# A two-pass graph layer on one core: loads issued ahead of ScalarE's sums, VectorE's share of the row sums from 5 to 4 groups of 16, and long and short stripes in turn in the second pass

## The chip, the cores and the metric

The kernel runs on one core of a Trainium2 chip. The metric is the device time of one execution in microseconds (us), lower is better. A change of under about 0.2% can't be told from no change here.

## The reference

Only this much of it matters (N = 8192 rows, 128 features, all float32):

```python
def _L0_gnn_ref(x, adj, W):
    A_hat = adj + jnp.eye(adj.shape[0], dtype=adj.dtype)
    d_inv_sqrt = jnp.sum(A_hat, axis=1) ** (-0.5)
    A_norm = d_inv_sqrt[:, None] * A_hat * d_inv_sqrt[None, :]
    support = x @ W.T
    out = A_norm @ support
    return jax.nn.relu(out)
h = jnp.maximum(_layernorm(x, axis=-1), 0.0)
x = x + _L0_gnn_ref(h, adj, L0_gnn_W)
return x
```

The matrix adj is 8192 x 8192 float32, 268 MB, and can't be kept on the chip. A row of the output needs the row sums of all columns' rows (the factor on the right), so a block of adj can enter the product only when the sums of the rows with its columns' numbers are known.

## The kernel before, in words

**Cells and stripes.** The rows are cut into 16 stripes u of 512 rows. A stripe and a column group v (512 columns) meet in a cell (u, v) of 1.05 MB: 128 partitions with 16 groups (C = 16) of 128 values each. A whole stripe is 16.8 MB. A cell is transposed by VectorE in two halves (L663, `adjT<-...`), and TensorE then does four 128x512 products with it (L460), each of which the trace records as two MATMUL rows, since the data is float32.

**First pass.** For each stripe in turn all its 16 cells are read, since its row sums need them all. The cells are of three kinds. `far` cells (right of the band, v > u+2) are only summed, and dropped. `left` cells (v < u) are summed and also multiplied, since the sums of their column's rows are known. `near` and `thirds` hold the three cells of the band (v = u, u+1, u+2), which are kept on the chip and multiplied later, each column of them when its scale is known.

**Second pass.** The far cells of stripes 0 to 12 (91 of the 256) are read again (`again` pieces), in the order of stripes that AGAIN_ROWS gives, and multiplied. A stripe that is complete is turned back, scaled, rectified, added to x and stored, while the next ones run (`finish`, `rows_back`, `combine`, `relu`, and a last addition on GpSimd).

**Pieces and slots.** far, left and again cells arrive in numbered pieces m of at most 3 cells' worth in three buffers, slot0 to slot2, in turn (in the second pass `thirds` is a fourth). Half of every piece (quarters 0 and 1 of the partitions) is loaded from SyncE's DMA queue, the other half (quarters 2 and 3) from ScalarE's. `load_piece(queue, quarters, m)` first waits, then issues. SyncE does nothing but these loads and the stores. ScalarE issues its halves between its sums: `next_piece(m)` issues its half of piece m + 2, and after the last piece of a stripe the halves of near and thirds (L292, L298), which wait for VectorE's transposes of older band cells.

**Who sums what.** A far piece is summed by ScalarE alone (L504). In left pieces and in near VectorE sums the first DVE_C of the 16 groups (L648), ScalarE the others, one instruction a group (L515, a 3-cell group is 128x384). A left slot is free when ScalarE has summed it (`act_freed`) and VectorE has transposed and summed it (`dve_freed`).

**End of a stripe.** ScalarE sums near, raises `act_sums` (L564), and VectorE folds the sums (`fold_parts`, L683 to L693), TensorE adds them over partitions (L431), VectorE, GpSimd (L389) and VectorE make the scale and scale support. Only then may the column's band cells be multiplied. In stripes 1 to 8 these band cells stand ahead of the stripe's left cells in the product order, in stripes 9 to 15 up to four left cells stand ahead of them.

**ScalarE's queue.** Instructions of an engine run in the order of the code, its DMA issues included. An issue that has to wait holds up the sums behind it.

Of the kernel before, what the change touches and what calls it, by code (L numbers as in the profile page):

```python
# [28 lines left out]
def gnn_kernel(nc: bass.Bass, x: bass.AP, adj: bass.AP, w: bass.AP, out: bass.AP):  # L29
# [13 lines left out]
    AHEAD = 2  # L43
    HALVES = 2
    TURNS = 3
    BANKS = 5
    DVE_C = 5
    FIRST = 4
    JUNKS = 3
    XC = 4  # L50
# [1 line left out]
    EPS = 1e-5  # L52
    CHAIN_X = 6
    FAR_ROWS = NB - 1 - BAND
    AGAIN_ROWS = [0] + list(reversed(range(1, FAR_ROWS)))

    adj_v = adj.rearrange("(bb u r) (b j) -> u b r bb j", bb=B, u=NB, b=B)
    adj_far = adj.rearrange("(bb u r) (b j) -> u r bb b j", bb=B, u=NB, b=B)
# [33 lines left out]
    AGAIN = len(landing)  # L92
    for u in AGAIN_ROWS:
        again[u] = []
# [12 lines left out]
    by_act = [sum(landing[k][0] != "again" for k in range(m + 1)) for m in range(len(landing))]  # L107
# [18 lines left out]
    stripe_at[NB] = len(order)  # L126
    rest = [(u, v, m) for u in AGAIN_ROWS for m in again[u] for v in range(landing[m][2], landing[m][2] + landing[m][3])]
    order += rest[:FIRST]
# [3 lines left out]
    def group(u, v):  # L132

        return u if v <= u + BAND else NB + AGAIN_ROWS.index(u)

# [6 lines left out]
    masked_by = [sum(2 if far[k] or k == FAR_ROWS else 1 for k in range(u + 1)) for u in range(NB)]  # L142
    finals = [u for u in range(FAR_ROWS, NB)] + AGAIN_ROWS

# [8 lines left out]
    with ctx:  # L153
# [6 lines left out]
        def sem(name):  # L160
            return ctx.enter_context(nc.semaphore(name))
# [53 lines left out]
        act_freed, dve_freed = sem("act_freed"), sem("dve_freed")  # L215
# [13 lines left out]
        def piece(m):  # L229

            n = landing[m][3]
            return slot[slot_of[m]][:, :C * n * CELL].rearrange("p (c j) -> p c j", c=C)

        def far_block(m):
            kind, u, bb, n, v, cells = landing[m]
            return slot[slot_of[m]][:, :n * B * cells * CELL].rearrange("p (a k) -> p a k", a=n)
# [26 lines left out]
        def transposed(n):  # L263

            return HALVES * (n + 1)

        def load_piece(queue, quarters, m):

            before = before_in_slot[m]
            if AHEAD <= m < AGAIN + AHEAD:  # L270
                queue.wait_ge(act_freed, by_act[m - AHEAD])
            if before is None:
                if slot_of[m] == SLOTS:
                    queue.wait_ge(t_done, transposed(column_at[NB - 1] + BAND))
            elif landing[before][0] == "again":
                kind, u, v, n = landing[before][:4]
                queue.wait_ge(t_done, transposed(place[u, v + n - 1]))
            else:
                queue.wait_ge(act_freed, by_act[before])
                if landing[before][0] == "left":  # L280
                    queue.wait_ge(dve_freed, by_dve[before])
            if landing[m][0] == "far":
                load_far(queue, quarters, m)
            else:
                load_cells(queue, quarters, m)
# [196 lines left out]
        @block.scalar  # L482
        def _(act):
            def layernorm(b):
                act.wait_ge(stats_ok, b // (TX // R) + 1)
                if b >= 2:
                    act.wait_ge(hT_ps, b - 1)
                for r in range(R):
                    t = b * R + r
                    nc.scalar.activation(h[b % 2][:, r, :], support[:, t, :], ACT.Relu, bias=shift[:, t:t + 1],  # L490
                                         scale=rstd[:, t:t + 1]).then_inc(h_ok, 1)

            def next_piece(m):

                load_piece(act, (2, 3), m + AHEAD)
                if m + AHEAD in last_piece:
                    load_kept(act, (2, 3), last_piece[m + AHEAD])

            def far_sums(m):
                u = landing[m][1]  # L500
                act.wait_ge(ld_slot[slot_of[m]], landed[m])
                for a in range(landing[m][3]):
                    at = landing[m][2] + a + (B if landing[m][4] > u + BAND + 1 else 0)
                    ins = nc.scalar.activation(far_block(m)[:, a, :], far_block(m)[:, a, :], ACT.Copy,  # L504
                                               accum_out=far_sum[u % 2][:, at:at + 1])
                ins.then_inc(act_freed, 1)
                next_piece(m)

            def late_sums(cells, u, k, before):
                n = cells.shape[2]  # L510
                for c in range(DVE_C, C):
                    at = before * (C - DVE_C) + c - DVE_C
                    if at >= JUNKS:
                        act.wait_ge(junk_done, at - JUNKS + 1)
                    nc.scalar.activation(junk[at % JUNKS][:, :n], cells[:, c, :], ACT.Copy,  # L515
                                         accum_out=part[u % 2][:, k, c:c + 1]).then_inc(junk_done, 1)

            def left_sums(m, k, before):
                act.wait_ge(ld_slot[slot_of[m]], landed[m])
                late_sums(piece(m), landing[m][1], k, before)  # L520
                act.wait_ge(junk_done, (before + 1) * (C - DVE_C))
                act.sem_inc(act_freed, 1)
                next_piece(m)

            def keep(u):
                act.wait_ge(used, transposed(last_of[u]))
                nc.scalar.activation(acc[:, u, :], bank[u % BANKS][:], ACT.Copy).then_inc(kept_acc, 1)

            def relu(n):
                act.wait_ge(y_sum, n + 1)  # L530
                for r in range(R):
                    t = finals[n] * R + r
                    ins = nc.scalar.activation(y[n % 2][:, r, :], y[n % 2][:, r, :], ACT.Relu, scale=dinv[:, t:t + 1])  # L533
                ins.then_inc(y_ok, 1)

            for q in range(XC):
                for b in (2, 3):
                    act.dma_start(support[b * Q:(b + 1) * Q, q * TX:(q + 1) * TX, :],
                                  x_v[b, :, q * TX:(q + 1) * TX, :]).then_inc(ld_x[q], 16)
            for m in range(AHEAD):  # L540
                load_piece(act, (2, 3), m)
            act.wait_ge(ident_ok, 9)
            summed = 0
            for s in range(NB):
                if s >= 2:
                    act.wait_ge(total_ok, s - 1)
                if s == 0:
                    for b in range(NB):
                        layernorm(b)
                        if b % 4 == 3:  # L550
                            far_sums(far[0][b // 4])
                    for m in far[0][NB // 4:]:
                        far_sums(m)
                else:
                    for m in far[s]:
                        far_sums(m)
                for k, m in enumerate(left[s]):
                    left_sums(m, k, summed)
                    summed += 1
                act.wait_ge(ld_near[s % 2], 16 * B * (s // 2 + 1))  # L560
                late_sums(near[s % 2][:, :, :min(2, NB - s) * CELL], s, len(left[s]), summed)
                summed += 1
                act.wait_ge(junk_done, summed * (C - DVE_C))
                act.sem_inc(act_sums, 1)  # L564
                if s >= BAND + 1:
                    keep(s - BAND - 1)
            rectified = stored = 0
            for m in range(AGAIN + AHEAD, len(landing)):
                while rectified < done_by(m):
                    relu(rectified)  # L570
                    rectified += 1
                while stored < done_by(m - 1):
                    store(act, (2, 3), stored)
                    stored += 1
                load_piece(act, (2, 3), m)
                if slot_of[m] == SLOTS and before_in_slot[m] is None:
                    load_xin(act, (2, 3), 0)
                    load_xin(act, (2, 3), 1)
            while stored < NB:
                if rectified < NB:  # L580
                    relu(rectified)
                    rectified += 1
                store(act, (2, 3), stored)
                stored += 1
# [3 lines left out]
        def _(dve):  # L588
# [61 lines left out]
            def transposes(n):  # L650
# [14 lines left out]
                if m is not None and v == landing[m][2] + landing[m][3] - 1:  # L665
                    if landing[m][0] == "left":
                        early_sums(piece(m), u, left[u].index(m), DVE_C).then_inc(dve_freed, 1)

            def kept_sums(u):
                n = min(2, NB - u)  # L670
                dve.wait_ge(ld_near[u % 2], 16 * B * (u // 2 + 1))
                ins = early_sums(near[u % 2][:, :, :n * CELL], u, len(left[u]), DVE_C)
                if u + BAND < NB:
# [148 lines left out]
```

## Time and profile before

| | |
|---|---|
| time, median of 3 runs | 1297.64 us (1297.23 to 1299.93) |
| profiled execution's own time | 1299.58 us |
| its span, first to last instruction | 1297.8 us |
| TensorE busy | 987.8 us (76%) |
| VectorE busy | 842.5 us (65%) |
| ScalarE busy | 531.8 us (41%) |
| moved by DMA | 377.11 MB, mean 291 GB/s |
| granted TensorE clock, mean | 0.894 |

The profile gives busy times, waits and what ended them, the chain of work that ended last, and DMA rates, for the whole span or for a stretch of it. The median is 1.9 us under the profiled execution's time. The first far piece of stripes 1 to 9 lands at about 92, 140, 189, 237, 288, 340, 397, 451 and 507 us, and the second pass runs from about 975 us to the end.

### The profile page before, as it was taken

The numbers are of one execution on the slowest core, as the hardware profiler recorded it, in microseconds if no ns is written. First come the engines' busy times: TensorE is split into PE (matmuls) and PEld (weight loads), VectorE is DVE, ScalarE is ACT, GpSimd is POOL, SyncE is SP. The second block draws the span as 40 slices with busy tenths as digits, with TensorE's granted clock in tenths as the row PEclk, the third lists the DMA queues.
The fourth block names the chain that finished last, engine by engine and source line by source line (L and its number), as shares of the span: only waits on it lengthen the run. The fifth ranks groups of instructions, "written<-read, shape, count | busy, mean of one in ns | idle before, by whom it ended". The sixth has DMA issues, their size and how long they took to land.

```text
span 1297.8 us, 8958 instructions
## 1 busy us (share of the span) xinstructions
PE 987.8 (76%) x2363; PEld 450.4 (35%) x2363; DVE 842.5 (65%) x958; ACT 531.8 (41%) x1596; POOL 52.6 (4%) x61
## 2 busy tenths in 40 slices
PE   1632334755767675678898999899999989999997
PEld 0531112322323232333343444344444434444443
DVE  5441342554646655676788888788877767777775
ACT  2875654753746537182646453654401100000000
POOL 3000000000000000000000000000000110000000
PEclk9866766877888988789898999999999999999999
DMA  9589999999999998999999999998969999999991
GB/s 307 224 291 335 365 325 338 340 323 292 323 323 295 338 267 265 274 274 287 268 312 272 297 252 250 291 304 256 272 165 312 302 326 320 324 340 299 331 318 27
DMA packets 289858, 377.11 MB, mean 291 GB/s; under 512 B 11152, under 2 KB 269328, under 8 KB 289808
## 3 DMA queue, kind: packets, MB, share of 16 engines
q1 hardware_dynamic: 144976, 188.31, 49.7%
q10 hardware_dynamic: 144832, 188.24, 48.1%
q8 instruction: 19, 0.31, 0.1%
q14 instruction: 31, 0.25, 0.1%
HBM read 372.31 MB, written 4.19 MB: 290 GB/s over the span
## 4 chain that ended last, share of the span: by engine, by line
PE 35%; DMA 29%; ACT 14%; ACTq 8%; issue 7%; DVE 5%; SPq 2%; POOLq 0%; POOL 0%; DVEq 0%
PE bank L460 34%; DMA slot<-in_adj_dram 27%; ACT junk L515 8%; ACTq L298 5%; ACT slot L504 5%; DVE adjT L663 4%; DMA thirds<-in_adj_dram 2%; ACTq L251 1%; ACTq L259 1%; ACT acc L490 1%; ACTq L292 1%; SPq L332 1%; DVE part L648 1%; SPq L251 1%; PE pre L443 0%
## 5 line engine op out<-in xcount | busy, mean ns | idle before, releaser
L460 PE MATMUL bank<-adjT,support 128*128 128x512 f32 x2048 | 942.5, 621 | 215.2 <-DVE adjT L663 215.2
L460 PEld LDWEIGHTS bank<-adjT,support 128*128 128x128 f32 x2048 | 403.3, 200 | 731.5 <-issue 725.2
L663 DVE STREAM_TRANSPOSE adjT<-slot 128x1024 f32<-128x1024 f32 x380 | 458.9, 1230 | 294.4 <-DMA slot<-in_adj_dram 204.9
L515 ACT ACTIVATE junk<-slot 128x384 bf16<-128x384 f32 (+2 forms) x495 | 233.4, 473 | 285.6 <-issue 128.0
L504 ACT ACTIVATE slot<-slot 128x6144 f32<-128x6144 f32 (+11 forms) x56 | 166.3, 2970 | 91.3 <-DMA slot<-in_adj_dram 54.1
L533 ACT ACTIVATE near<-near,dinv 128x128 f32<-128x128 f32 x64 | 20.2, 390 | 337.4 <-DVE adjT L663 140.2
L663 DVE STREAM_TRANSPOSE adjT<-near 128x1024 f32<-128x1024 f32 x62 | 76.6, 1239 | 34.0 <-PE bank L460 34.0
L663 DVE STREAM_TRANSPOSE adjT<-thirds 128x1024 f32<-128x1024 f32 x70 | 84.6, 1231 | 17.1 <-PE bank L460 11.2
L515 ACT ACTIVATION_READ_ACCUMULATOR junk<-slot 128x1 f32 x495 | 92.4, 187 | 0.0
L648 DVE TENSOR_REDUCE part<-slot 128x5 f32<-128x1920 f32 (+2 forms) x45 | 85.0, 1890 | 0.0
L515 ACT ACTIVATE junk<-near 128x256 bf16<-128x256 f32 (+1 forms) x176 | 69.3, 395 | 19.6 <-issue 13.3
L389 POOL TENSOR_TENSOR dinv<-total,power 128x4 f32<-128x4 f32 x16 | 16.1, 1007 | 847.5 <-DVE total L711 847.5
L410 PE MATMUL bank<-ident,acc 128*128 128x128 f32 x64 | 14.0, 359 | 33.9 <-ACT acc L490 33.9
L431 PE MATMUL sums_bank<-by_block,spread 128*128 128x64 f32 x32 | 7.4, 320 | 39.7 <-DVE by_block L693 39.7
L648 DVE TENSOR_REDUCE part<-thirds 128x16 f32<-128x2048 f32 x14 | 31.9, 2278 | 2.4 <-DMA thirds<-in_adj_dram 2.3
L398 POOL TENSOR_TENSOR near<-near 128x512 f32<-128x512 f32 x16 | 20.2, 1267 | 327.4 <-ACT near L533 283.6
L515 ACT ACTIVATION_READ_ACCUMULATOR junk<-near 128x1 f32 x176 | 32.9, 187 | 0.0
L490 ACT ACTIVATE acc<-support,acc 128x128 f32<-128x128 f32 x64 | 25.3, 479 | 9.6 <-issue 7.0
L418 PE MATMUL bank<-acc 128*128 128x128 f32 x128 | 21.8, 327 | 9.3 <-DVE acc L616 9.3
L648 DVE TENSOR_REDUCE part<-near 128x5 f32<-128x1280 f32 (+1 forms) x16 | 22.9, 1434 | 5.0 <-DMA near<-in_adj_dram 5.0
L616 DVE COPY acc<-bank 128x512 f32<-128x512 f32 x16 | 10.9, 689 | 20.4 <-PE bank L410 20.2
L418 PEld LDWEIGHTS bank<-acc 128*128 128x128 f32 x128 | 20.4, 241 | 9.9 <-DVE acc L616 9.9
(54 smaller groups left out, 174.3 us busy)
## 6 DMA issues: line engine op xcount, KB each, us to landing
slot<-in_adj_dram SPq DMA_DIRECT2D x100, 768.0 KB, 12.6
slot<-in_adj_dram ACTq DMA_DIRECT2D x100, 768.0 KB, 13.9
slot<-in_adj_dram SPq DMA_DIRECT2D x48, 512.0 KB, 10.3
slot<-in_adj_dram ACTq DMA_DIRECT2D x48, 512.0 KB, 11.5
near<-in_adj_dram SPq DMA_DIRECT2D x30, 512.0 KB, 14.4
near<-in_adj_dram ACTq DMA_DIRECT2D x30, 512.0 KB, 15.6
slot<-in_adj_dram ACTq DMA_DIRECT2D x8, 1536.0 KB, 11.4
slot<-in_adj_dram SPq DMA_DIRECT2D x8, 1536.0 KB, 10.2
```

The lines of the kernel that those rows point to most:

```text
L251: queue.dma_start(piece(m)[b * Q:(b + 1) * Q, :, :], adj_v[u, b, :, :, v * CELL:(v + n) * CELL]).then_inc(ld_slot[slot_of[m]], 16)
L298: queue.dma_start(third[u % 3][b * Q:(b + 1) * Q, :, :], adj_v[u, b, :, :, (u + 2) * CELL:(u + 3) * CELL]).then_inc(ld_third[u % 3], 16)
L389: nc.gpsimd.tensor_tensor(dinv[:, u * R:(u + 1) * R], total[:], power[:, :R], ALU.pow).then_inc(root_ok, 1)
L398: nc.gpsimd.tensor_tensor(o[n % 2], y[n % 2], xin[n % 2], ALU.add).then_inc(o_ok, 1)
L418: ins = nc.tensor.matmul(sup_bank[b % 2][:, r * D:(r + 1) * D], hT[b % 2][:, r * P:(r + 1) * P], wT[:], start=True, stop=True)
L460: ins = nc.tensor.matmul(bank[g % BANKS][:], support[:, v * R + t, :], adjT[at % TURNS][:, r, :], start=(n == first_of[g] and t == 0), sto ...
L490: nc.scalar.activation(h[b % 2][:, r, :], support[:, t, :], ACT.Relu, bias=shift[:, t:t + 1], scale=rstd[:, t:t + 1]).then_inc(h_ok, 1)
L504: ins = nc.scalar.activation(far_block(m)[:, a, :], far_block(m)[:, a, :], ACT.Copy, accum_out=far_sum[u % 2][:, at:at + 1])
L515: nc.scalar.activation(junk[at % JUNKS][:, :n], cells[:, c, :], ACT.Copy, accum_out=part[u % 2][:, k, c:c + 1]).then_inc(junk_done, 1)
L533: ins = nc.scalar.activation(y[n % 2][:, r, :], y[n % 2][:, r, :], ACT.Relu, scale=dinv[:, t:t + 1])
L648: return nc.vector.tensor_reduce(part[u % 2][:, k, :most], cells[:, :most, :], AX.X, ALU.add)
L663: nc.vector.transpose(adjT[at % TURNS][:].rearrange("p t (c i) -> p t c i", i=Q), half.rearrange("p c (t r) -> p t c r", r=Q)).then_inc(t_ ...
```

## The change

Three things are changed. The two that stand in the loads go together. (1) The wait of both queues for ScalarE's sums of piece m - 2 is gone, so piece m waits only for its slot, which piece m - 3 held. On ScalarE `next_piece(m)` now stands behind the wait for piece m's landing and ahead of its sums. (2) DVE_C is 4 in place of 5, so ScalarE sums 12 of 16 groups of left pieces and near. (3) AGAIN_ROWS becomes 0, 12, 1, 11, 2, 10, 3, 9, 4, 8, 5, 7, 6 in place of 0, 12, 11, ..., 1. The whole difference:

```diff
-    DVE_C = 5
+    DVE_C = 4
@@
-    AGAIN_ROWS = [0] + list(reversed(range(1, FAR_ROWS)))
+    AGAIN_ROWS = [k // 2 if k % 2 == 0 else FAR_ROWS - 1 - k // 2 for k in range(FAR_ROWS)]
@@ def load_piece
             before = before_in_slot[m]
-            if AHEAD <= m < AGAIN + AHEAD:
-                queue.wait_ge(act_freed, by_act[m - AHEAD])
             if before is None:
@@ def far_sums
                 act.wait_ge(ld_slot[slot_of[m]], landed[m])
+                next_piece(m)
                 for a in range(landing[m][3]):
...
                 ins.then_inc(act_freed, 1)
-                next_piece(m)
@@ def left_sums
                 act.wait_ge(ld_slot[slot_of[m]], landed[m])
+                next_piece(m)
                 late_sums(piece(m), landing[m][1], k, before)
                 act.wait_ge(junk_done, (before + 1) * (C - DVE_C))
                 act.sem_inc(act_freed, 1)
-                next_piece(m)
```

Lines of the changed kernel behind L270 have smaller numbers by 2, in `far_sums` and after it by 1 or 2.

On ScalarE, stripe 3, from its second far piece (in slot1) on, before. `slot` rows with 5120 values are the sums of a far piece, DMA rows with L259 issue a far piece, with L251 a left one:

```order
L504 ACTIVATE slot1,far_sum1<-slot1 128x5120
L259 DMA slot0<-in_adj_dram 128x2x1280
L504 ACTIVATE slot2,far_sum1<-slot2 128x5120
L251 DMA slot1<-in_adj_dram 32x16x384 x2
L292 DMA near1<-in_adj_dram 32x16x256 x2
L298 DMA thirds<-in_adj_dram 32x16x128 x2
L504 ACTIVATE slot0,far_sum1<-slot0 128x5120
L259 DMA slot2<-in_adj_dram 128x2x1152
```

And the same place after the change:

```order
L259 DMA slot0<-in_adj_dram 128x2x1280
L503 ACTIVATE slot1,far_sum1<-slot1 128x5120
L251 DMA slot1<-in_adj_dram 32x16x384 x2
L290 DMA near1<-in_adj_dram 32x16x256 x2
L296 DMA thirds<-in_adj_dram 32x16x128 x2
L503 ACTIVATE slot2,far_sum1<-slot2 128x5120
L259 DMA slot2<-in_adj_dram 128x2x1152
L503 ACTIVATE slot0,far_sum1<-slot0 128x5120
```

Each issue has moved over one piece's sums, and the six issues at the end of the stripe (left, near, thirds) now stand ahead of the sums of the third-last piece (slot2), with three pieces' sums behind them instead of two.

On TensorE, in the second pass, behind the end of stripe 0. L460 is the product, four a cell, and L443 turns a finished stripe back. Before:

```order
L460 MATMUL bank<-adjT,support 128x512 x4
L443 MATMUL pre<-ident,near 128x128 x4
L460 MATMUL bank<-adjT,support 128x512 x8
L443 MATMUL pre<-ident,near 128x128 x4
L460 MATMUL bank<-adjT,support 128x512 x12
L443 MATMUL pre<-ident,near 128x128 x4
L460 MATMUL bank<-adjT,support 128x512 x16
L443 MATMUL pre<-ident,near 128x128 x4
L460 MATMUL bank<-adjT,support 128x512 x20
```

And after the change:

```order
L458 MATMUL bank<-adjT,support 128x512 x4
L441 MATMUL pre<-ident,near 128x128 x4
L458 MATMUL bank<-adjT,support 128x512 x48
L441 MATMUL pre<-ident,near 128x128 x4
L458 MATMUL bank<-adjT,support 128x512 x8
L441 MATMUL pre<-ident,near 128x128 x4
L458 MATMUL bank<-adjT,support 128x512 x44
L441 MATMUL pre<-ident,near 128x128 x4
L458 MATMUL bank<-adjT,support 128x512 x12
```

Stripes of 1, 2, 3, 4 and 5 cells in a row have become 1, 12, 2, 11 and 3. The number of products is the same.

## Rows read from the trace of the kernel before

**Rows 1.** The page: busy time of the engines, and GB/s in 40 slices of the span.
```profile
PE 987.8 (76%) x2363; PEld 450.4 (35%) x2363; DVE 842.5 (65%) x958; ACT 531.8 (41%) x1596; POOL 52.6 (4%) x61
...
GB/s 307 224 291 335 365 325 338 340 323 292 323 323 295 338 267 265 274 274 287 268 312 272 297 252 250 291 304 256 272 165 312 302 326 320 324 340 299 331 318 27
```

**Rows 2.** Windows of stripes 1 to 8, and the second pass.
```profile
core 0: us, PE busy (x) PEld busy (x) DVE busy (x) ACT busy (x) POOL busy (x), PEclk, DMA share, GB/s
...
92.00:140.00 48.00, 11.35 (x20) 5.02 (x20) 11.58 (x21) 29.48 (x52) 2.02 (x2) 0.64 1.04 353
140.00:189.00 49.00, 20.31 (x36) 8.73 (x36) 15.60 (x18) 28.99 (x53) 0.00 (x0) 0.67 1.00 337
189.00:237.00 48.00, 26.34 (x48) 10.98 (x48) 20.71 (x22) 28.92 (x54) 1.01 (x1) 0.70 1.03 350
237.00:288.00 51.00, 31.03 (x60) 13.36 (x60) 26.27 (x32) 30.34 (x76) 1.01 (x1) 0.75 1.03 318
288.00:340.00 52.00, 33.75 (x68) 14.65 (x68) 27.65 (x28) 28.62 (x70) 1.01 (x1) 0.79 1.00 317
340.00:397.00 57.00, 36.86 (x78) 16.34 (x79) 31.64 (x36) 31.18 (x82) 1.01 (x1) 0.82 0.98 327
397.00:451.00 54.00, 39.62 (x84) 16.61 (x83) 33.49 (x33) 30.42 (x97) 1.01 (x1) 0.91 1.04 299
451.00:507.00 56.00, 42.94 (x92) 18.43 (x92) 37.05 (x37) 30.34 (x98) 1.01 (x1) 0.91 1.04 304
...
975.00:1298.00 323.00, 303.95 (x740) 135.57 (x740) 227.34 (x238) 20.23 (x64) 20.20 (x16) 0.98 0.99 289
```

**Rows 3.** Waits of TensorE in 92:503 (two rows), 503:700, 700:975, 975:1298.
```profile
PE bank L460 <- DVE adjT L663: 140.9, 19, 23.4
PE sums_bank L431 <- DVE by_block L693: 28.5, 7, 9.1
...
PE bank L460 <- DVE adjT L663: 51.1, 6, 25.5
...
PE bank L460 <- DVE adjT L663: 10.5, 5, 4.4
...
PE bank L460 <- DVE adjT L663: 12.7, 8, 2.7
```

**Rows 4.** The chain of work, stripe 1: start us, us, what.
```profile
82.01 10.91 DMA slot<-in_adj_dram
...
92.97 5.21 issue
...
98.39 10.29 DMA slot<-in_adj_dram
...
117.82 4.16 ACTq L298
```

**Rows 5.** Timeline of ScalarE in stripe 7: start us, us, what.
```profile
400.10 2.75 ACT L504 ACTIVATE slot<-slot 128x3072 f32<-128x3072 f32 x1
402.97 1.53 ACTq L251 DMA_DIRECT2D slot<-in_adj_dram  x2
...
419.42 1.44 ACTq L251 DMA_DIRECT2D slot<-in_adj_dram  x2
...
427.01 6.65 ACTq L298 DMA_DIRECT2D thirds<-in_adj_dram  x2
```

**Rows 6.** DMA rate in 40 slices of 1.35 us, stripe 7 (397:451).
```profile
GB/s 401 401 401 360 61 95 259 229 212 225 289 239 232 210 228 286 351 269 249 217 266 241 349 357 370 332 335 344 347 344 296 292 300 247 366 396 394 396 394 396
```

**Rows 7.** Groups of instructions, shapes apart: a sum's cost.
```profile
L504 ACT ACTIVATE slot<-slot 128x6144 f32<-128x6144 f32 x8 | 42.5, 5318 | 23.9 <-DMA slot<-in_adj_dram 16.0 <-issue 7.9
...
L515 ACT ACTIVATE junk<-slot 128x384 bf16<-128x384 f32 x341 | 173.0, 508 | 212.2 <-issue 96.9 <-DMA slot<-in_adj_dram 70.7 <-DVE adjT L663 43.3
...
L515 ACT ACTIVATE junk<-slot 128x256 bf16<-128x256 f32 x143 | 57.2, 401 | 72.9 <-issue 31.1 <-DVE adjT L663 27.2 <-DMA slot<-in_adj_dram 13.2
...
L648 DVE TENSOR_REDUCE part<-slot 128x5 f32<-128x1920 f32 x31 | 65.5, 2112 | 0.0
```

**Rows 8.** Waits of VectorE in 92:529: for the landing, and for ScalarE's sums.
```profile
DVE adjT L663 <- DMA slot<-in_adj_dram: 157.4, 14, 26.2
...
DVE folded L683 <- ACTq L564: 8.7, 6, 2.7
```

**Rows 9.** Waits of SyncE's queue in the second pass.
```profile
SPq L311 <- POOL near L398: 70.4, 5, 28.5
```

## The prediction

> **What bounds the kernel now.** I read the slices of the page first, then the same stretch stripe by stripe, then TensorE's waits, and last the chain through one stripe.
>
> The page [rows 1] has no engine that is busy throughout: TensorE 76%, and the DMA engines move 291 GB/s on average where single slices reach 368. So the kernel has stages with different limits. [rows 2] shows them. In stripes 1 to 8 TensorE is busy 11 to 43 us of 48 to 57, and the data comes at 353 down to 299 GB/s. In the second pass it is busy 304 of 323 us, and there the DMA has time left. What TensorE waits for [rows 3] agrees: before 503 us 140.9 + 28.5 us, from 503 to 700 us 51.1, from 700 to 975 us 10.5 and in the second pass 12.7. Nearly all of it ends with a transpose of VectorE, and VectorE itself waits there for the landing of a slot (157.4 us up to 529 us [rows 8]). So up to about 700 us the kernel is bound by when pieces land, and after that by TensorE. A microsecond won before 700 us moves everything behind it forward, and one won on loads after that is worth little.
>
> Why do pieces land late? The chain [rows 4] shows the pattern: a piece travels (10.91 us), ScalarE sums it (5.21 us, shown as issue), and only then the next but one is issued and travels (10.29 us). The sum stands between two transfers. In stripe 7 [rows 5] the far piece's sums end at 402.85, and ScalarE issues its half of the next left piece at 402.97; that one's sums lead to the issue at 419.42. What this costs in rate is in [rows 6]: from 404 to 418 us, with little in flight, 210 to 290 GB/s, and where the last left piece, near and thirds are queued together 330 to 370, at the same busy share near 1.0 [rows 2]. The busy share doesn't tell that the DMA is at its limit. A second hold is the issue itself: the last two issues of a stripe occupy ScalarE for 6.65 us [rows 5] (4.16 us in stripe 1 [rows 4]), since the queue takes them only as earlier ones are drained, while landed pieces lie unsummed.
>
> **The change part by part.**
>
> Loads ahead of sums. SyncE's half of piece m now waits for the slot that piece m - 3 held, up to one piece's sum earlier. ScalarE's half of m + 2 goes out when piece m lands, not when it is summed. Not every such step pays. After the last landing of a stripe ScalarE has the sums of three pieces and near ahead of it instead of two and near, because the six issues at the stripe's end have moved ahead of the third-last piece's sums. So the loads at a stripe's start stay about where they were, relative to that landing, and what is taken out of the stripe's cycle is one sum: that of the third-last piece. From 5.32 us for 6144 values [rows 7] I estimate by size 5.3, 4.9, 4.5, 4.0, 3.6 and 3.2 us for stripes 1 to 6, where it is a far piece, and 11 x 0.401 = 4.4 us for stripes 7 and 8, where it is a left piece of 2 cells. The sum is 34.3 us.
>
> Against this stands the rate. A stripe is 16.8 MB. At 368 GB/s, the best slice [rows 1], it needs 45.6 us, so stripe 1 (48 us) can give 2.4 and stripe 3 (48 us) 2.4 and not 5.3 and 4.5; the others have room [rows 2]. That leaves 2.4 + 3.4 (49 us) + 2.4 + 4.0 + 3.6 + 3.2 + 4.4 + 4.4 = 27.8 us. It is not a hard limit, since the slices of stripe 7 reach 401 on far pieces [rows 6].
>
> In stripe 0 ScalarE is busy with the layernorm, and the first five pieces wait for it. Here SyncE's halves of pieces 2, 5 and 6 leave much earlier, and piece 7 no longer waits for the 5.2 us of sums ahead of it [rows 4]. I take 7 us, between 0 and the 10.4 us of two such sums.
>
> Stripes 9 to 11. TensorE waits 51.1 us between 503 and 700 us [rows 3], 25.5 of it in one piece at the start of stripe 9. That one waits for a piece whose issue is still behind near's sums on ScalarE's half, so I take 3 us of it. Of the other 25.6 us, which wait for left pieces whose loads stood behind a left piece's sums (11 x 0.508 = 5.6 us [rows 7]), I take half, 12. Together 15 us.
>
> From 700 us on. There are 10.5 + 12.7 us of waits left to win [rows 3]. Sums now come later at the end of each stripe, by one piece's sums (5.6 us) and the twelfth group. VectorE's fold waits for them (8.7 us in six waits, all before 529 us [rows 8]), and behind the fold stand the transposes. Between 529 and 975 us there was no such wait. I expect small ones, and put them at 0 net against the earlier loads.
>
> VectorE 4 groups for 5. VectorE saves a fifth of 2.112 us, 0.42 us, for each of 31 pieces of 3 cells, and by size 0.3 us for the other left pieces and near, about 21 us in all. It is busy 65% [rows 1], and where it is late it is because data or TensorE is, so this saves nothing but some tenths at the end of a stripe. ScalarE gets one instruction more for each left piece and near, 0.51 or 0.40 us [rows 7]. In stripes 1 to 8 these are 15 left pieces and 8 near, 23 x 0.45 = 10 us, on the engine whose sums free the slots. SyncE's half is ahead by a piece and hides part of it. I take half, 5 us. If nothing hides it, it is 10.
>
> Order of the second pass. The products are the same. SyncE's loads wait for stores 70.4 us in all, 28.5 at the longest [rows 9], where short stripes follow one another and so many finishes fall together. Spread out, they delay fewer loads, but TensorE waits only 12.7 us there [rows 3]. I take 2 us, with bounds 0 and 10.
>
> Sum: 7 + 27.8 - 5 + 15 + 0 + 2 = 46.8, say 47 us less. On the profiled execution 1299.6 - 47 = 1252.6, and the median stands 1.9 us lower, so **1250.7 us**, said as 1250.
>
> **The rivals.**
>
> *The rate is the limit (little gain).* If the DMA can't move more than it does because it is at its ceiling for these short runs, the earlier issues only lengthen the queue, and ScalarE stands longer in its own issues (6.65 us now [rows 5]) before the sums. For it speaks the busy share of about 1.0 in every stripe. Against it speak the 401 and 370 GB/s beside 212 in one stripe [rows 6]. What would be left is the 7 us of stripe 0, half of stripes 9 to 11 and the 2 us, less the 5 us: about -12 us, 1286. The Trainium skill, "DMA: Bandwidth & Descriptors", section "Specifications", gives about 358 GB/s as HBM's limit for a core. By that figure a stripe would need 46.9 us, and the 27.8 us above would be about 24 (an estimate from that page's figure). This trace disagrees: 368 GB/s over a whole slice [rows 1] and 401 over several short ones [rows 6], and the measurement decides.
>
> *Sums too late (slower).* In stripes 9 to 15 ScalarE waits, ahead of the sums of the third-last piece, for VectorE to transpose the band cells so that near may be loaded. Both the sums and the slot behind them hang on it. The stripe's sums are then complete 5.6 + 3 x 0.5 = 7 us later, and if the fold finds them missing each time, and TensorE runs through its three buffers of half a cell (`adjT`), seven stripes lose up to 7 us each, 49 us, which just eats the gain; with 10 us for the twelfth groups in place of 5, and some tenths more, it ends at 1297.6 - 47 + 49 + 6, about 1306. It decides when more than 6.7 us per stripe are really lost. Against it speaks that VectorE never waited for these sums between 529 and 975 us [rows 8], so there is slack, of unknown size.
>
> *More than the sum.* If the earlier half also lifts the rate in the middle of the stripes (370 for 212 to 290 in [rows 6]), the stripes go to 45 us: stripes 1 to 8 take 360 us for 415 (55 less), and with 7 and 15 us the time is about 1297.6 - 77, 1220.
>
> *Nothing changes*, because a slot's own wait binds everywhere. [rows 5] speaks against it: the issue follows ScalarE's last sum within 0.12 us.
>
> **How the numbers follow.** A gain of 25 to 70 us (1228 to 1273): 0.62. The rate as limit, 1273 to 1294: 0.16. More than the sum, under 1228: 0.12. Within 0.2%, which is about what a measurement of this kernel can tell from no change: 0.03. Slower: 0.07. So faster 0.90, same 0.03, slower 0.07. The range that leaves out 2 in 10 goes from 1222 to 1286: the low end is all of the 34.3 us, 10, 25 and 7, the high end the rival of the rate.
>
> **What would show it.** In the changed kernel's trace, the windows of stripes 1 to 8 should be 2 to 6 us shorter each, with rates of 340 to 360; the first far piece of stripe 9 should land at 475 to 485 us for 507. TensorE's waits for transposes before 700 us should fall from 192 to about 150 us, and from 700 us on stay near 23. ScalarE's issues should directly follow a landing, and the waits of `folded` for ScalarE's sums should grow from 8.7 us. Waits of `folded` of several us each in stripes 9 to 15 would show the second rival. Unchanged stripes with longer issues on ScalarE would show the first. In the second pass the longest wait of a store should be under 28 us. The prediction is wrong if stripe 9 begins later than 500 us.

## The result, and the profile after

The changed kernel takes 1267.6 us, median of 4 runs (1262.9 to 1271.0), against 1298.8 us before (1297.2 to 1300.8, 4 runs). The ratio is 0.9757 with a 95% interval of 0.9718 to 0.9795: 31 us less, where 47 were forecast. The profiled execution is the fastest of the four, 1262.9 us with a span of 1261.1, so its trace shows 36.7 us less than that of before. In the experiments below, a ratio leaves out the executions that lie more than 1.5% above the fastest of their kernel (three of six in e7, one of six in e5 and in e11), while a median is of all executions.

The page of the changed kernel, in the places of [rows 1], and the chain by engine, of the changed kernel and (last row) of before.

```profile
PE 983.5 (78%) x2363; PEld 450.9 (36%) x2363; DVE 826.4 (66%) x958; ACT 559.7 (44%) x1718; POOL 52.6 (4%) x61
...
GB/s 304 318 307 371 379 377 340 330 361 346 324 339 297 293 351 259 273 267 295 297 243 293 283 185 316 238 346 224 288 174 317 304 346 339 310 332 312 321 314 47
...
PE 46%; ACT 25%; DMA 11%; ACTq 10%; DVE 4%; issue 2%; SPq 1%; POOL 0%; POOLq 0%; DVEq 0%
...
PE 35%; DMA 29%; ACT 14%; ACTq 8%; issue 7%; DVE 5%; SPq 2%; POOLq 0%; POOL 0%; DVEq 0%
```

DMA's share of the chain fell from 29% to 11%, and that of ScalarE with its issues rose from 22% to 35%. Windows of the changed kernel follow, cut at the landings of the first far pieces of stripes 2 to 9, and the second pass (columns as in [rows 2]).

```profile
127.20:173.60 46.40, 20.21 (x36) 8.72 (x36) 15.79 (x21) 29.53 (x56) 1.01 (x1) 0.68 1.05 372
173.60:218.90 45.30, 26.71 (x52) 11.71 (x52) 21.21 (x25) 27.59 (x49) 1.01 (x1) 0.74 1.05 355
218.90:267.60 48.70, 29.92 (x60) 13.08 (x60) 24.36 (x28) 33.77 (x93) 1.01 (x1) 0.81 1.05 343
267.60:314.30 46.70, 31.13 (x68) 13.65 (x68) 26.96 (x30) 28.87 (x70) 1.01 (x1) 0.87 1.05 350
314.30:368.70 54.40, 38.25 (x76) 16.62 (x76) 30.16 (x32) 32.63 (x90) 1.01 (x1) 0.78 0.99 338
368.70:420.20 51.50, 37.98 (x84) 16.77 (x84) 33.20 (x35) 29.79 (x94) 1.01 (x1) 0.86 1.09 312
420.20:474.20 54.00, 41.19 (x92) 18.38 (x92) 36.36 (x37) 32.53 (x108) 1.01 (x1) 0.85 1.07 315
942.00:1261.00 319.00, 303.39 (x741) 136.33 (x740) 229.98 (x242) 20.34 (x64) 20.26 (x16) 0.98 1.00 294
```

Before, cut the same way, stripes 2 to 8 take 48.4, 47.7, 51.8, 51.4, 57.5, 53.5 and 56.6 us. Now they take 46.4, 45.3, 48.7, 46.7, 54.4, 51.5 and 54.0: 2.0 to 4.7 us less each, 19.9 in all. Stripe 2 begins at 127.2 us for 140.5, so stripes 0 and 1 gave 13.3. Nearly all of it is stripe 0: the first far piece of stripe 1 lands at 79.8 us for 92.9 (ScalarE, still in earlier sums, takes it up at 88.9), and stripe 1 then takes 47.4 us for 47.6. What TensorE waits for in 90:494 (two rows), 494:665, 665:942 (two rows) and 942:1261, the same work as in the stretches of [rows 3]:

```profile
PE bank L458 <- DVE adjT L661: 79.9, 16, 13.4
PE sums_bank L429 <- DVE by_block L691: 65.3, 7, 13.0
...
PE bank L458 <- DVE adjT L661: 46.8, 6, 21.8
...
PE bank L458 <- DVE adjT L661: 13.4, 6, 4.0
PE sums_bank L429 <- DVE by_block L691: 3.0, 1, 3.0
...
PE bank L458 <- DVE adjT L661: 8.0, 3, 5.2
```

The waits for transposes before stripe 9's cells fell from 140.9 to 79.9 us, but those for the folded sums (`by_block`) rose from 28.5 to 65.3. They hang on ScalarE, whose sums VectorE's fold waits for: 49.6 us in 90:494, where before it was 8.7 [rows 8]:

```profile
DVE adjT L661 <- DMA slot<-in_adj_dram: 87.6, 10, 19.3
DVE folded L681 <- ACTq L562: 49.6, 7, 10.5
```

Stripe 9's first product starts at 494.2 us, 34.8 earlier than the 529.0 of before. The wait of TensorE that ends there is 21.8 us for 25.5. From there to the end it is 766.9 us for 768.8. So nearly all was won before stripe 9, and next to nothing behind it.

### The profile page after: what moved, and what is told of

Read it like the earlier page. It is cut to its first block, busy times and chain, and to the rows that moved or that the text cites. A ratio compares the mean times of both kernels' runs of the same rounds, so it can differ in the third digit from the quotient of the medians.

```text
span 1261.1 us, 9000 instructions
## 1 busy us (share of the span) xinstructions
PE 983.5 (78%) x2363; PEld 450.9 (36%) x2363; DVE 826.4 (66%) x958; ACT 559.7 (44%) x1718; POOL 52.6 (4%) x61
## 3 DMA queue, kind: packets, MB, share of 16 engines
q1 hardware_dynamic: 144976, 188.31, 51.1%
q10 hardware_dynamic: 144832, 188.24, 50.3%
## 4 chain that ended last, share of the span: by engine, by line
PE 46%; ACT 25%; DMA 11%; ACTq 10%; DVE 4%; issue 2%; SPq 1%; POOL 0%; POOLq 0%; DVEq 0%
PE bank L458 44%; ACT junk L513 16%; DMA slot<-in_adj_dram 9%; ACT slot L503 8%; ACTq L296 5%; DVE adjT L661 3%; ACTq L290 2%; DMA thirds<-in_adj_dram 2%; ACTq L259 2%; ACTq L251 1%; DMA support<-in_x_dram 1%; PE bank L416 1%; PE bank L408 1%; DVE part L646 1%; SPq L330 1%
## 5 line engine op out<-in xcount | busy, mean ns | idle before, releaser
L513 ACT ACTIVATE junk<-slot 128x384 bf16<-128x384 f32 (+2 forms) x540 | 254.6, 473 | 230.0 <-issue 145.9
L513 ACT ACTIVATION_READ_ACCUMULATOR junk<-slot 128x1 f32 x540 | 100.9, 187 | 0.0
L661 DVE STREAM_TRANSPOSE adjT<-thirds 128x1024 f32<-128x1024 f32 x72 | 87.4, 1231 | 15.4 <-PE bank L458 12.4
L513 ACT ACTIVATE junk<-near 128x256 bf16<-128x256 f32 (+1 forms) x192 | 75.5, 394 | 2.7 <-ACT junk L513 2.7
L646 DVE TENSOR_REDUCE part<-slot 128x4 f32<-128x1536 f32 (+2 forms) x45 | 68.9, 1532 | 0.0
L681 DVE TENSOR_REDUCE folded<-part 128x16 f32<-128x96 f32 (+5 forms) x16 | 4.1, 254 | 56.3 <-ACTq L562 56.3
L429 PEld LDWEIGHTS sums_bank<-by_block,spread 128*128 128x128 f32 x32 | 7.0, 250 | 88.8 <-DVE by_block L691 85.4
L513 ACT ACTIVATION_READ_ACCUMULATOR junk<-near 128x1 f32 x192 | 35.8, 186 | 0.0
L416 PE MATMUL bank<-acc 128*128 128x128 f32 x128 | 21.8, 326 | 8.8 <-DVE acc L614 8.8
## 6 DMA issues: line engine op xcount, KB each, us to landing
slot<-in_adj_dram SPq DMA_DIRECT2D x98, 768.0 KB, 13.1
```

Of the source, the lines that this page charges most:

```text
L416: ins = nc.tensor.matmul(sup_bank[b % 2][:, r * D:(r + 1) * D], hT[b % 2][:, r * P:(r + 1) * P], wT[:], start=True, stop=True)
L646: return nc.vector.tensor_reduce(part[u % 2][:, k, :most], cells[:, :most, :], AX.X, ALU.add)
L661: nc.vector.transpose(adjT[at % TURNS][:].rearrange("p t (c i) -> p t c i", i=Q), half.rearrange("p c (t r) -> p t c r", r=Q)).then_inc(t_ ...
```

## The experiments

Times are medians, and ratios are to the kernel before, run beside them on the same chip. e1 to e4 stand in one group with the same runs of before, e5 to e8 in a second, e9 to e11 in a third; e12 and the changed kernel (0.9757) each have their own. Between groups compare ratios, not times.

| kernel | median us | ratio | 95% interval |
|---|---|---|---|
| e1: loads only | 1268.4 | 0.9766 | 0.9737 to 0.9795 |
| e2: share 4 only | 1306.9 | 1.0040 | 1.0018 to 1.0063 |
| e3: order only | 1296.0 | 0.9973 | 0.9956 to 0.9991 |
| e4: changed kernel, share 5 | 1263.2 | 0.9726 | 0.9702 to 0.9751 |
| e5: near and thirds behind the sums | 1273.0 | 0.9783 | 0.9747 to 0.9819 |
| e6: near and thirds from SyncE alone | 1312.4 | 1.0108 | 1.0070 to 1.0147 |
| e7: SyncE's loads ahead only | 1293.1 | 0.9842 | 0.9789 to 0.9894 |
| e8: ScalarE's loads ahead only | 1455.6 | 1.1182 | 1.1141 to 1.1223 |
| e9: e4, two left cells ahead of the band | 1261.8 | 0.9707 | 0.9677 to 0.9736 |
| e10: e4, near and thirds one piece later | 1278.3 | 0.9830 | 0.9797 to 0.9864 |
| e11: changed kernel, share 6 | 1255.9 | 0.9641 | 0.9604 to 0.9678 |
| e12: e11 and e9 together | 1251.6 | 0.9617 | 0.9581 to 0.9653 |

### The three edits apart: e1, e2, e3

e1 is the changed kernel with share and order put back:

```diff
-    DVE_C = 4
+    DVE_C = 5
-    AGAIN_ROWS = [k // 2 if k % 2 == 0 else FAR_ROWS - 1 - k // 2 for k in range(FAR_ROWS)]
+    AGAIN_ROWS = [0] + list(reversed(range(1, FAR_ROWS)))
```

> Only the loads are changed: the wait for piece m - 2 is gone and ScalarE issues ahead of its sums; VectorE still sums 5 of 16 groups and the second pass has its old order. Theory A (the gain is all from earlier loads before stripe 9, and the two other edits cost or give little): 30 to 38 us under the kernel before, so as fast as the changed kernel or up to 5 us faster, and stripe 9's first left piece lands near 490 us. Theory B (VectorE's smaller share is part of the gain, since VectorE stands between landing and product): only 15 to 28 us under before.

e2 is the kernel before with only its `DVE_C = 5` made 4:

> The kernel before with VectorE's share 4 of 16 groups instead of 5, nothing else. Theory A: ScalarE's sums are between two transfers there, so 23 more instructions of 0.40 to 0.51 us in stripes 1 to 8 cost about 10 us, 1.005 to 1.010 of before. Theory B: VectorE's 21 us less give 3 to 10 us, 0.992 to 0.998.

e3 is the kernel before with only its AGAIN_ROWS replaced by the new line:

> The kernel before with long and short stripes in turn in the second pass, nothing else. Theory A: TensorE is busy there in any case, 0 to 4 us less, within 0.3% of before. Theory B (order is a real part of the gain): 6 to 10 us less, with TensorE's waits after 975 us falling from 12.7 us to under 5.

Measured: -2.3%, +0.4% and -0.3%, that is about -30, +5 and -4 us of 1299. In e1 stripe 9's first left piece lands at 493.2 us. Theory A holds for e1 and e3. For e2 it has the direction, and 1.0040 lies a little under its 1.005 to 1.010, with an interval that reaches into it. Theory B (VectorE's smaller share is part of the gain) falls with e2. The loads are the whole gain. The three add up to -29 us, the changed kernel has -31, within the intervals.

### The share in the changed kernel: e4, e11

e4 is the changed kernel with `DVE_C = 5`, e11 with `DVE_C = 6`.

> The changed kernel with VectorE's share put back to 5 of 16 groups. Theory A (in the changed kernel the sums of ScalarE set the pace of stripes 1 to 8, its share of the chain is 25% after 14%): 3 to 8 us faster than the changed kernel, 1255 to 1264 us. Theory B: 5 us or more slower than the changed kernel.

> The changed kernel with VectorE's share 6 of 16 groups. From 4 to 5 the time fell by about 4 us. Theory A (ScalarE's sums set the pace before stripe 9): another 2 to 5 us less than with share 5, 0.969 to 0.972 of before, and VectorE's waits for ScalarE's sums fall below 35 us. Theory B (VectorE's own time now counts): the same as share 5 or slower.

Shares 4, 5 and 6 give 0.9757, 0.9726 and 0.9641. From 4 to 5 the two intervals overlap. From 5 to 6 they don't (0.9702 to 0.9751 and 0.9604 to 0.9678, of two groups), and 0.9641 is under the 0.969 to 0.972 of theory A, which had the direction right. e1 and e4 differ only in the order of the second pass: 0.9766 and 0.9726 in one group, with intervals that overlap. VectorE's wait for ScalarE's sums in the whole trace is 56.3 us in the changed kernel, then in e4

```profile
DVE folded L681 <- ACTq L562: 42.4, 9, 6.9
```

and in e11

```profile
DVE folded L681 <- ACTq L562: 29.6, 9, 6.1
```

Each group that VectorE takes over cuts 13 to 14 us from that wait. VectorE gets longer by 0.4 us a 3-cell piece, and up to 6 groups the time doesn't rise by it. So the change moved the share in the wrong direction.

### One queue ahead, the other not: e7, e8

e7 is the kernel before without the wait in `load_piece`; ScalarE still issues behind its sums:

```diff
-            if AHEAD <= m < AGAIN + AHEAD:
-                queue.wait_ge(act_freed, by_act[m - AHEAD])
```

> The kernel before, with only the wait for piece m - 2 taken out. It holds SyncE's halves earlier by up to a sum; ScalarE still issues behind its sums. If the half that comes last decides when a piece may be used (theory A: the gain needs both halves): 0 to 8 us under before. If a fuller queue is enough (theory E): 15 us or more under before.

e8 is e1, but SyncE keeps the wait:

```diff
+            if quarters[0] == 0 and AHEAD <= m < AGAIN + AHEAD:
+                queue.wait_ge(act_freed, by_act[m - AHEAD])
```

> Loads as in the changed kernel on ScalarE's queue only; SyncE still waits for the sums of piece m - 2. Share 5 and the old order, so to be held against the loads-only kernel at 0.977 of before. Theory A: as with the other half alone, 0 to 10 us under before, since SyncE's halves land last. Theory E: 15 us or more under before.

e7 stays open between the theories. Its six executions run from 1273.0 to 1316.0 us, wider than any other kernel's. The ratio of 0.9842 (20 us less, as theory E has it) rests on the three lowest, and the median of all six, 1293.1 us, is 6 us under that of before (theory A). The trace, of an execution of 1296.9 us, shows why both can be read from it. Stripe 9's first left piece lands at 502.9 us for 527.6 before, 24.7 earlier, where e1 with both halves ahead has 34.4. But the first left piece of stripe 12 lands at 689.7 for 697.3, so 17 of the 24.7 us are lost again in stripes 9 to 11, in this execution. No run here shows what loses them.

e8 is 11.8% slower, 153 us, and no theory had that. Its timeline of ScalarE in stripe 7, behind two far pieces:

```profile
472.32 1.27 ACTq L251 DMA_DIRECT2D slot<-in_adj_dram  x2
473.63 1.85 ACTq L292 DMA_DIRECT2D near<-in_adj_dram  x2
475.52 6.94 ACTq L298 DMA_DIRECT2D thirds<-in_adj_dram  x2
482.51 0.42 ACT L515 ACTIVATE junk<-slot 128x256 bf16<-128x256 f32 x1 [13.62 <-DVE adjT L663]
487.20 1.12 ACTq L259 DMA_DIRECT2D slot<-in_adj_dram  x2
```

and that of SyncE's queue (the six loads of the stripe's three left pieces, then near):

```profile
461.69 26.65 SPq L251 DMA_DIRECT2D slot<-in_adj_dram  x6
488.38 6.90 SPq L292 DMA_DIRECT2D near<-in_adj_dram  x2
```

ScalarE issues its half of the last left piece at 472.3, then stands in near and thirds until 482.5, sums the third-last piece, and only at 487.1 SyncE's wait for these sums ends and the other half leaves (the last two of the six issues), 15 us later. A piece is there when both halves are. The hold of ScalarE, which cost little where no load hung on it, is now between two loads of every stripe. 153 us over 15 stripes are 10 us each on average; by the landings of the first far pieces, stripes 1 to 11 take 4 to 20 us more each than before. This is the mechanism of the prediction's second rival, with a load hung on the late sums instead of the fold.

### ScalarE's hold at a stripe's end: e5, e6

e5 splits `next_piece`: the kept loads go behind the sums again.

```diff
+            def next_kept(m):
                 if m + AHEAD in last_piece:
                     load_kept(act, (2, 3), last_piece[m + AHEAD])
@@ far_sums, left_sums, as their last line
+                next_kept(m)
```

> The changed kernel, but at a stripe's end ScalarE issues only the last left piece ahead of its sums; its halves of near and thirds go behind the sums of the third-last piece, as before the change. Theory C (in the changed kernel ScalarE stands in these issues while landed pieces lie unsummed, and that took the 12 us expected in stripes 9 to 11): 5 to 15 us faster than the changed kernel, 1250 to 1262 us, and VectorE's waits for ScalarE's sums fall from 56 us to under 40. Theory D (the near data is needed early, or these stripes are bound elsewhere): the same as the changed kernel within 3 us, or slower.

e6 gives all quarters to SyncE, and takes them from ScalarE:

```diff
-                    load_kept(sp, (0, 1), last_piece[m])
+                    load_kept(sp, (0, 2, 1, 3), last_piece[m])
@@ next_piece
-                if m + AHEAD in last_piece:
-                    load_kept(act, (2, 3), last_piece[m + AHEAD])
```

> The changed kernel, with all four quarters of near and thirds loaded from SyncE's queue, so ScalarE never stands in them. Theory C: 10 to 25 us faster than the changed kernel, since ScalarE's hold at each stripe's end is gone altogether. Theory D: slower, since SyncE's queue then carries twice as much there in a row and its halves of the next pieces come late behind it.

Theory C falls, since it had both kernels faster than the changed one, and theory D holds. In e5 VectorE's wait for the sums fell from 56.3 to 33.2 us, as it said, and the time didn't follow: 0.9783, its interval overlaps the changed kernel's. In e6 that wait is 1.1 us, and the kernel is slower than before. SyncE's queue in stripes 4 and 5 of e6 shows why:

```profile
238.02 7.37 SPq L251 DMA_DIRECT2D slot<-in_adj_dram  x4
245.45 12.22 SPq L290 DMA_DIRECT2D near<-in_adj_dram  x4
257.72 12.89 SPq L296 DMA_DIRECT2D thirds<-in_adj_dram  x4
270.65 13.80 SPq L259 DMA_DIRECT2D slot<-in_adj_dram  x4
```

Eight DMAs occupy it for 25 us, and its half of the next far piece leaves at 270.65, where ScalarE's half left at 250.87. The hold is the queue's, not ScalarE's: put on one queue it delays that queue's halves of the next pieces.

### Stripes 9 to 11: e9, e10

Before and after, stripe 9's first left piece lands 50.3 us ahead of stripe 10's (527.6 and 577.9; 492.7 and 543.0), and in e1, e2, e3, e4 and e5 it is 50 to 52 us. near's load may be what sets that. Timeline of SyncE's queue, before (stripe 9, that piece lands at 527.6):

```profile
548.00 1.26 SPq L292 DMA_DIRECT2D near<-in_adj_dram  x2
549.30 1.66 SPq L298 DMA_DIRECT2D thirds<-in_adj_dram  x2
557.12 1.91 SPq L259 DMA_DIRECT2D slot<-in_adj_dram  x4
```

and in the changed kernel (it lands at 492.7):

```profile
513.48 1.26 SPq L290 DMA_DIRECT2D near<-in_adj_dram  x2
514.78 1.62 SPq L296 DMA_DIRECT2D thirds<-in_adj_dram  x2
522.86 1.91 SPq L259 DMA_DIRECT2D slot<-in_adj_dram  x4
```

near leaves 20.4 and 20.8 us after the landing, and the next stripe's first piece 29.5 and 30.2. near waits for VectorE's transposes of band cells, which stand behind four left cells at TensorE's pace. SyncE's wait for them there, in the changed kernel and before:

```profile
SPq L290 <- DVE adjT L661: 20.7, 1, 20.7
...
SPq L292 <- DVE adjT L663: 13.4, 1, 13.4
```

The earlier loads only made it 7 us longer. e9 is e4 with two of them:

```diff
-        before = 0 if NB - 1 - s - BAND > 4 else min(FIRST, max(0, s - 1))
+        before = 0 if NB - 1 - s - BAND > 4 else min(2, max(0, s - 1))
```

> The changed kernel with share 5, and in stripes 9 to 15 two left cells stand ahead of the band's cells instead of four. From stripe 9 on every kernel so far takes the same time per stripe (50 to 52 us from stripe 9's to stripe 10's first left piece). Theory F: that time is set by the load of near, which waits for VectorE's transposes of the band cells, which go at TensorE's pace behind four left cells; two cells fewer are 6.9 us less per stripe in stripes 9 to 11: 10 to 20 us faster than the share-5 kernel (0.973 of before), 0.957 to 0.966. Theory G (DMA rate or ScalarE's sums set it, and the scale of the stripe isn't ready two cells earlier): same as the share-5 kernel, or up to 15 us slower, with TensorE waiting for by_block.

e10 is e4 with the kept loads of stripes 9 to 14 one piece later on both queues:

```diff
-        last_piece = {(far[u] + left[u])[-1]: u for u in range(NB)}
+        last_piece = {(far[u] + left[u])[-1] + (9 <= u < NB - 1): u for u in range(NB)}
```

> The changed kernel with share 5, and in stripes 9 to 14 both queues issue near and thirds one piece later, behind the first piece of the next stripe, so that this piece doesn't stand behind near's wait. Theory F: the next stripe's first piece is issued 10 us or more earlier after the landing of stripe 9's first left piece (now 30 us after it), and the time falls by 8 to 25 us against the share-5 kernel, 0.954 to 0.967 of before. Theory G: within 4 us of the share-5 kernel, since the bytes are the same and near is then what comes late.

In e9 the piece lands at 489.9, near leaves at

```profile
504.19 1.26 SPq L290 DMA_DIRECT2D near<-in_adj_dram  x2
...
514.25 1.91 SPq L259 DMA_DIRECT2D slot<-in_adj_dram  x4
```

which is 14.3 us after it, where e4 has 21.4, and the next piece 24.4, where e4 has 30.3. The stripe's 52.2 us (e4) became 46.8, and stripe 12's first left piece lands at 652.9 for 663.4. So near's wait does set when the loads of these stripes leave. But the time is 0.9707 for 0.9726, about 2 us and within the intervals, and not the 10 to 20 us of theory F. TensorE's waits in 529:700 are, in e4,

```profile
PE bank L458 <- DVE adjT L661: 27.8, 6, 7.8
```

and in e9

```profile
PE bank L458 <- DVE adjT L661: 21.2, 6, 10.6
```

and in 700:975 they rose from 13.4 to 15.9 us. Loads 10.5 us earlier left TensorE with 4 us less to wait. Theory F is right on the loads and wrong on the time. e10 issues the next piece 13 us after the landing, but near not earlier (514.03 us, 21.4 after it), and it is 1% slower than e4, with 39.0 us of TensorE's waits in 529:700 for 27.8. Both theories expected less than that: F had it 8 to 25 us faster, G within 4 us. The likely reading is that the stripe needs near and thirds too, and that late kept cells cost more than a late far piece; no run takes that apart.

### The best of them together: e12

e12 has share 6 and two left cells ahead of the band.

> Share 6 and two left cells ahead of the band, with the changed loads and order. With two cells the loads of stripe 12 came 10 us earlier but the time fell by 4 us at the most. Theory H (from stripe 12 on TensorE sets the pace and swallows what is won on loads in stripes 9 to 11): again 0 to 5 us under the share-6 kernel, 0.960 to 0.965 of before, though stripe 12's first left piece lands 8 us or more earlier than the 657 us there. Theory I (the smaller hold in ScalarE lets it through): 8 us or more under the share-6 kernel.

0.9617 against e11's 0.9641 is theory H, though the intervals, of two groups, don't tell the two apart. Stripe 12's first left piece lands at 648.7 for 657.4 us. It is the fastest version, 3.8% under before and about 1.4% under the changed kernel.

## Why the prediction came out as it did

The direction was right, and so was where the gain comes from: loads ahead before stripe 9. The size was a third too large (31 us measured, 47 forecast), and the term for stripes 9 to 11 is the one that failed.

**Loads ahead in stripes 0 to 8.** The prediction had 7 us for stripe 0, 27.8 less 5 for stripes 1 to 8, and 3 for stripe 9's first piece: 32.8. The trace shows 34.8 at the first product of stripe 9. That the two are so close is in part luck. Stripe 0 gave 13.1 us for 7, more than the 10.4 set as its bound. Stripe 1 gave 0.2 for 2.4, and stripes 2 to 8 gave 19.9 us for 20.4 (25.4 less the 5), of which stripes 7 and 8 gave 2.0 and 2.6 for 4.4 each. The way from there to stripe 9's first product gave 1.6, for 3. A sign that was named, ScalarE's issues directly behind a landing, isn't there either: after the first far piece of stripes 1 to 9 its next issue comes 2.7 to 8.6 us late, behind sums that it still has to do. And TensorE's waits moved in part: those for transposes before stripe 12 fell further than forecast (from 192.0 us to 126.7, where about 150 was said), but those for the folded sums rose by 36.8 us, which the sum had not priced. Its sentence that the sum of the third-last piece is what leaves the cycle is not proved by that, since e5 moves the kept loads behind these sums again and stays near the same time.

**Stripes 9 to 11.** This is the step that failed: "of the other 25.6 us, which wait for left pieces whose loads stood behind a left piece's sums, I take half, 12". In the stretch 494:665 TensorE waits 46.8 us for 51.1, so without the first wait 25.0 for 25.6. From stripe 9's first left piece to stripe 12's it is 170.7 us for 169.7, so these stripes didn't get shorter at all. The loads there stood behind near's wait for the band's transposes (SyncE's in stripe 9 is 20.7 us for 13.4), and a sum taken out of ScalarE's queue doesn't move that. e9 shows that wait: cut by 7 us, it brings stripe 12 10.5 us earlier, but TensorE only 4 us less of waits and the time about 2 us, not clear of noise. So even earlier loads would have paid little there.

**From 700 us on.** Put at 0 net, and measured so: the waits of TensorE in 665:942 and 942:1261 are 24.4 us with the folded sums, for 23.2 [rows 3]. The second rival expected up to 7 us of waits for late sums in each of stripes 9 to 15. There is one wait of VectorE for them in 494:942, of 5.1 us, and one of 3.0 us of TensorE for the fold. The same late sums are waited for in stripes 1 to 8 instead (49.6 us of VectorE).

**VectorE's share.** Put at +5, measured +5.2 (e2). In the changed kernel e4 has about the same, 4 us, which is not clear of noise there; 6 groups for 4 are (e11).

**Order.** Put at -2, measured -3.5 (e3, 0.9 to 4.4 less in 1000). SyncE's longest wait for a store fell from 28.5 to 19.3 us, as expected, but the sum of these waits is 76.9 us for 70.4.

**The rivals.** "The rate is the limit" is refuted for whole stripes by stripes 2 to 5 at 343 to 372 GB/s, where 315 to 349 stood, and by the time. "More than the sum" falls too: the rate in the middle of stripe 7 did not rise. The DMA engines' busy share and the rate in 40 slices of 368.7:420.2 of the changed kernel, to hold against [rows 6], and (last row) the busy share before, in the slices of [rows 6]:

```profile
DMA  9999999999999999999999999999999999999999
GB/s 401 401 410 340 193 209 213 215 226 211 212 228 215 231 323 349 286 240 218 355 363 364 359 360 341 338 348 348 344 309 295 292 278 323 373 395 388 398 394 398
...
DMA  9999139999999999999999999999999999999999
```

What is gone is the hole: the two slices at 61 and 95 GB/s, in which the engines were busy for about 1 and 3 tenths of the time. The stretch at 193 to 231 is still there, and it is not for want of loads, as the prediction read it ("with little in flight"). From 379.3 to 387.0 us both of the stripe's left pieces of two cells are on their way, the engines are busy throughout, and the rate is 221 GB/s; packets of 1024 bytes take 83 ns each there, and 52 ns between 401 and 405 us, where it is near 345. So in this stretch the first rival has a point: earlier loads didn't raise the rate. That fits stripes 7 and 8, which gave about half of what was forecast. Why the packets are slower there is not settled.

The forecast was 46.8 us and the traces show 36.7, which is 2.0 more up to stripe 9's first product and 12.1 less behind it (1.9 us for 14). The medians show 31.2, another 5.5 less, since both profiled executions lie off their medians (1262.9 for 1267.6, and 1299.6 for 1298.8). No step of the sum explains that part.

## What to carry to other kernels

Where a load is split over two queues, look at the later half: advancing one queue gave between 0.4% and 1.6% and a wide scatter, advancing the other alone cost 11.8%, and both together gave 2.3%. Don't put an issue that can block ahead of work that another queue's load waits for. A wait that vanishes moves the bound to the next wait in the same cycle, so read for each stage which one that is (here near's load from stripe 9 on) before taking a share of the stage's idle time. And when a change makes one engine's queue the chain, look at shares that move work to or from it: here the share went the wrong way, and 6 groups for 4 gave another 1.2%.

## What of the hardware was not expected

A DMA issue on ScalarE or SyncE is not free while earlier ones of its queue are under way. Two issues took 6.65 us [rows 5], and eight in a row on SyncE 25.1 us (e6). In the kernel before, the issues of left pieces, near and thirds between 30 and 700 us took 0.6 to 0.8 us on average when up to three earlier ones of the same queue had not landed (145 issues), 2.2 us with four (48) and 4.6 us with five (15). The busy share of the DMA engines stood near 1.0 both at 212 and at 401 GB/s, so it tells a hole (the digits 1 and 3 above) but not the rate: the same 1024-byte packets took 52 ns in one stretch and 83 ns in another, at the same busy share.
